# State-space block of a two-layer decoder: the rows of a state are spread two states ahead of their use, and the low-rank rows are copied ahead of the decays

## The reference

```python
xz = layernorm(x) @ W_in;  x_in, z = split(xz)
xc = silu(causal_conv4(x_in) @ pw_kernel + conv_bias)         # 512 inner channels
x_dbl = xc @ W_x                                              # 16 + 8 + 8 columns
delta = softplus(x_dbl[..., :16] @ W_dt + b_dt)
Bm, C = x_dbl[..., 16:24], x_dbl[..., 24:]                    # 8 states
h[t]  = exp(delta[t] * A) * h[t-1] + delta[t] * Bm[t] * xc[t] # per channel and state
y[t]  = sum over the 8 states of C[t] * h[t]
x = x + ((y + xc * D) * silu(z)) @ W_out
```

## Time and profile before

| what | us |
|---|---|
| median of three runs | 3070.16 |
| the profiled execution, own time | 3073.5 |
| its span | 3071.7 |
| state-space groups, first scan to last gating | about 105 to 774 |
| TensorE busy, whole span | 2722.0 (89%) |
| VectorE busy, whole span | 1997.4 (65%) |
| ScalarE busy, whole span | 1518.1 (49%) |
| mean granted TensorE clock | 0.928 |

### The profile page before, as it was taken

One profiled execution on the slowest core, in us unless ns is written; L12 is line 12 of the kernel. 1 busy time (PEld: TensorE's weight loads), 2 busy tenths in 40 slices (PEclk: granted clock), 3 DMA queues, 4 the chain that ended last, 5 costly groups with the idle time before them and its releaser, 6 DMA issues. The chain is left out here.

```text
span 3071.7 us, 60127 instructions
## 1 busy us (share of the span) xinstructions
PE 2722.0 (89%) x20702; PEld 1767.6 (58%) x20703; DVE 1997.4 (65%) x4542; ACT 1518.1 (49%) x2982; POOL 454.4 (15%) x482
## 2 busy tenths in 40 slices
PE   6899999996799999999876689999999799969993
PEld 3344444443466676766665347777777645556662
DVE  2588888888367777777555447777777555653334
ACT  2666666663156666666443136666666233302222
POOL 0000000000300000000033111000110032324441
PEclk9899999997899999999877789999999899969997
DMA  4000000000100000000000100000000120001225
GB/s 112 0 1 0 0 0 0 0 0 0 35 21 20 20 15 20 20 20 15 1 15 1 39 11 26 20 20 20 20 25 11 49 83 20 14 26 61 63 61 165
DMA packets 57938, 80.70 MB, mean 26 GB/s; under 512 B 8880, under 2 KB 47059, under 8 KB 57491
## 3 DMA queue, kind: packets, MB, share of 16 engines
q1 hardware_dynamic: 51778, 62.69, 7.2%
q0 software_dynamic: 6048, 16.52, 1.7%
HBM read 63.59 MB, written 15.60 MB: 26 GB/s over the span
## 5 line engine op out<-in xcount | busy, mean ns | idle before, releaser
L1120 DVE CUSTOM_DVE_ANT_0 xa_h_scores<-xa_h_score_bank,xa_h_added 112x375 f32<-112x375 f32 x1024 | 518.1, 544 | 148.5 <-PE xa_h_score_bank L1055 133.6
L1214 ACT ACTIVATE xa_h_probs<-xa_h_scores,xa_h_negmax 112x375 f32<-112x375 f32 x1024 | 561.4, 600 | 0.9 <-DVE xa_h_negmax L1127 0.6
L1067 PEld LDWEIGHTS xa_h_turn_bank<-keep_ident,xa_h_probs 112*125 112x125 f32 x3072 | 398.6, 190 | 91.4 <-DVE xa_h_probs_t L1134 22.2
L1067 PE MATMUL xa_h_turn_bank<-keep_ident,xa_h_probs 112*125 112x112 f32 x3072 | 438.5, 279 | 8.8 <-DVE xa_h_probs_t L1134 8.5
L1134 DVE COPY xa_h_probs_t<-xa_h_turn_bank 125x448 f32<-125x448 f32 x512 | 319.1, 623 | 150.9 <-PE xa_h_turn_bank L1067 137.6
L1220 ACT ACTIVATE xa_h_probs_t<-xa_h_turn_bank 125x448 f32<-125x448 f32 x256 | 138.6, 541 | 304.5 <-PE xa_h_turn_bank L1067 304.5
L464 PE MATMUL mb_y_bank<-mb_read_out,keep_ident 128*128 128x448 f32 x512 | 231.7, 601 | 30.3 <-DVE mb_read_out L671 30.3
L664 DVE TENSOR_TENSOR_SCAN mb_state<-mb_decay,mb_drive 128x1792 f32<-128x1792 f32 x64 | 253.8, 3965 | 0.2 <-ACT mb_decay L598 0.2
L1055 PE MATMUL xa_h_score_bank<-xa_h_keys,xa_h_queries 32*112 32x375 f32 x2048 | 231.6, 522 | 11.3 <-DVE xa_h_row_max L1120 10.7
L1080 PEld LDWEIGHTS xa_h_sums_bank<-xa_h_probs_t,xa_h_values 125*32 125x32 f32 x6144 | 141.9, 110 | 154.5 <-DVE xa_h_probs_t L1134 149.2
L1080 PE MATMUL xa_h_sums_bank<-xa_h_probs_t,xa_h_values 125*32 125x112 f32 x6144 | 202.7, 265 | 14.6 <-issue 7.3
(11 more groups left out here) (341 smaller groups left out, 4145.7 us busy)
## 6 DMA issues: line engine op xcount, KB each, us to landing
xa_context<-in_ctx_t SPq DMA_DIRECT2D x64, 375.0 KB, 3.1
lm_w<-in_m_w SPq DMA_DIRECT2D x16, 512.0 KB, 9.9
lm_e_wide<-lm_result_rows SPq DMA_DIRECT2D x8, 896.0 KB, 9.8
keep_x<-in_x SPq DMA_DIRECT2D x4, 896.0 KB, 16.0
lm_latent_rows<-lm_rows SPq DMA_DIRECT2D x8, 448.0 KB, 3.2
out_x<-keep_x SPq DMA_DIRECT2D x8, 448.0 KB, 6.3
xa_mask_raw<-in_key_mask SPq DMA_DIRECT2D x1, 1312.5 KB
mb_f_pw<-in_pw SPq DMA_DIRECT2D x1, 1024.0 KB
```

The costliest lines, as they stand in the source:

```text
L1067: last = pe.transpose(turn_bank[(par + kc) % 2][0:KP, g * S:(g + 1) * S], probs[par][:, g, kc * KP:(kc + 1) * KP], keep.ident[0:S, 0:S])
L1120: dve.tensor_tensor_reduce(scores[par][:, g, :], score_bank[g][0:S, 0:SK], added[s][:, :], 1.0, -BIG, ALU.add, ALU.max, row_max[par][:, g: ...
L1214: act.activation(probs[par][:, g, :], scores[par][:, g, :], ACT.Exp, bias=negmax[s][:, G * c + g:G * c + g + 1]).then_inc(probs_ready, 1)
```

## The change

On TensorE each spread moves. The spread of state n + 1 no longer opens turn n; the spread of state n + 2 is issued in turn n instead, after the turn's other matmuls and just before `add_state(g, n)`. So that this starts right, the next group's state 1 is spread at the end of turn 7, behind the second half of the projection, and for group 0 before the groups begin. On ScalarE `read_low` moves from behind `decays(g, n + 2)` to before it, in turn 5. The number of instructions of each kind stays what it was.

```diff
@@ TensorE, group
                 for n in range(N):
-                    if n + 1 < N:
-                        spread(g, n + 1)
                     if n == 0:
                         gate(g)
...
                             spread(g + 1, 0)
                         project_out(g, 1) if not first else pass_over(OUT_B)
+                        if not final:
+                            spread(g + 1, 1)
+                    if n + 2 < N:
+                        spread(g, n + 2)
                     add_state(g, n)
...
             spread(0, 0)
+            spread(0, 1)
             all_groups(pe, group)
@@ ScalarE, group
                         if not final:
                             read_rows(g)
+                    if n == 5 and not final:
+                        read_low(g)
                     if n + 2 < N:
                         decays(g, n + 2)
...
                     if n == 4:
                         read_inner(g, (2, 3))
-                    if n == 5:
-                        read_low(g)
                     if n == 6:
                         cast_first(g)
                         softplus(g)
```

## The result

The changed kernel takes 3046.2 us in the median of four runs (3037.34 to 3051.94), the kernel before 3070.51 us (3066.61 to 3071.97). The ratio is 0.9921, 95% interval 0.9907 to 0.9935: 24.3 us less, where 24.1 were forecast.

A forecast was written before the change was run, and what follows sets the result against it. TensorE was taken to bound the middle groups' states 1 to 4, the read-out-to-product round trip the last group. Savings of 11.2 + 6 x 2.05 + 0.65 = 24.1 us from 3070.2 gave 3046 us, range 3032 to 3060.

The forecast's parts named there:

- Last group: Push leaves the read-out-to-product round trip; scans start 7.65 us apart, 46.6 us from scan 1 to 7; 11.2 us saved.
- States 1 to 4: Middle groups: TensorE bounds at 9.40 us a state in either order, nothing saved; product's row wait near zero in states 3 to 6.
- Group 0: First group, without projection: delta already comes near the logarithm's end, so only softplus starting 0.65 us earlier counts.
- States 5 to 7 of the middle groups: Rows come earlier, low-rank's wait of 0.44 goes, delta starts at the logarithm's end: 2.05 us saved in each of six groups.
- From delta to the gates of the next group the chain is unchanged: Seam between groups: nothing changes there, so each of groups 1 to 6 keeps its 2.05 us, 12.3 in all.
- TensorE loses its clock at the seam: Rival, chance 0.05: longer idling between groups holds half clock through gates to push, 8.1 us a group, giving 3101 us.
- The early low copy: Low-rank result copied ahead of decays, else the spread of state 7 sits behind 1.28 + 2.33 us of exponentials.
- The 331.7: Trace time in us forecast for ScalarE's first copied row of state 7, behind the delayed decays; the product would start there.
- The added wait: TensorE's spread of the next group's state 1 waits 0.9 us for ScalarE's state 0 copy, seven times, hidden.
- The sum: Whole kernel: 11.2 + 6 x 2.05 + 0.65 = 24.1 us saved, so 3046 us.

The follow-up runs named there:

- the two kernels with idle matmuls: Three fp32 matmuls nobody reads before the second half of the gates, groups 0 to 5: on the changed kernel 3039.75 us, on the kernel before 3061.2 us.
- before, last group changed: The kernel before with the spreads ahead of the push in the last group alone, low copy left late: 3056.4 us, ratio 0.9949.
- changed, again: The changed kernel itself, unaltered, measured once more beside the later experiments: 3047.25 us, ratio 0.9928.
- with the spread behind the push: The changed kernel with the spread of the next group's state 1 issued after the push of state 7: 3050.18 us, ratio 0.9923.

## Why the prediction came out

*Last group: right.* Forecast 46.6 us from scan 1 to scan 7, measured 46.5; 11.2 saved, measured 11.9, the tail being 0.6 shorter, as much as the push of state 6 took less (5.71 for 6.34). TensorE's half clock does not matter between the scans, as said.

*States 1 to 4: right.* 9.40 us a state in both, no gain. Only the sign given for it was off: the product's wait for rows did not go near zero there.

*Group 0: right in size.* From first delta to gating 87.67 us before, 87.02 after: 0.65. The run with the low copy late shows that it could have been 1.2 more: the early copy costs that much here.

*States 5 to 7 of the middle groups: the mechanism right, slightly too small.* Forecast 2.05, measured 2.3 (84.98 to 82.64 and 82.71), and 1.8 to 2.25 between the two kernels with idle matmuls. Delta did move to the logarithm's end, 1.66 of the 2.3, and the rows of state 7 were not the last to come. The other 0.6 is low-rank's wait for the row copy: it was priced at its recorded 0.44, but before, low-rank started 0.99 us after the spread in front of it began, where 0.38 is what a spread takes.

*The step that failed is "From delta to the gates of the next group the chain is unchanged".* In waits it is, in clock not. The second half of the gates went from 3.27 to 6.11 in group 1 and from 4.97 to 6.2 or 6.3 in groups 3 and 5, and cost those groups 3.4, 1.7 and 1.7 us (the last two: 1.3 in the gates and 0.4 between low-rank and delta, 21.2 us for 20.84). So the six middle groups gave 7.1 us in the profiled execution where 12.3 were forecast: 5 x 2.3 + 2.5 = 14.0 by the order, less 6.8 by the clock. That the order itself was priced well is shown by the two kernels with idle matmuls, where the gates take 3.2 to 3.3 us on both sides: 11.8 us for groups 1 to 6 against the forecast of 12.3.

The rival "TensorE loses its clock at the seam" named the place, with a price far too high, as the level is back by the end of the gates. Its reason, a longer wait there, isn't borne out. The wait is longer in group 3 alone (3.18 for 2.57); in groups 1, 2 and 4 it is shorter, in group 5 the same, and the five together are 14.4 us in both traces. Wait before the second half of the gates / its length, in us, for three traces of each order:

| trace | group 1 | group 2 | group 3 | group 4 | group 5 | gates above 3.27, sum |
|---|---|---|---|---|---|---|
| before | 3.52 / 3.28 | 2.75 / 4.97 | 2.57 / 4.97 | 2.40 / 4.97 | 3.18 / 4.97 | 6.8 |
| before, low copy early | 3.52 / 4.97 | 3.18 / 3.27 | 2.71 / 4.97 | 2.52 / 4.97 | 2.35 / 4.97 | 6.8 |
| before, last group changed | 3.52 / 4.97 | 3.18 / 3.27 | 2.67 / 4.97 | 2.49 / 4.97 | 3.18 / 4.97 | 6.8 |
| changed | 3.21 / 6.11 | 2.48 / 4.89 | 3.18 / 6.23 | 2.31 / 4.97 | 3.18 / 6.31 | 12.2 |
| changed, again | 3.40 / 3.28 | 3.18 / 4.67 | 3.18 / 6.12 | 2.46 / 4.90 | 3.18 / 6.24 | 8.9 |
| changed, low copy late | 3.06 / 4.91 | 3.18 / 6.24 | 2.29 / 4.97 | 3.18 / 6.32 | 2.25 / 4.97 | 11.1 |

In these traces the gates always lose more in the new order than in the old one (the two traces not shown, with the last group in the old order and with the spread behind the push, have 11.9 and 11.7), so the loss comes with the order. The idle matmuls show that it needs the wait. Why the same wait costs more in the new order stays open.

*The early low copy.* Forecast: without it the spread of state 7 would sit behind 1.28 + 2.33 us of exponentials. That was wrong. The lead that the other edit gives lets ScalarE finish the decays first; with or without the copy ahead the time of the middle groups is the same, and group 0 pays 1.2 us for it. The 331.7 that I worked out for the first row was right. Counted from the start of low-rank it is 7.93 us by the forecast and 7.94 in the trace (324.42 to 332.36), and it is the decays, as forecast, that the row copy stands behind: they end at 331.90, while the spread of 330.88 was done at 331.42. With the low copy late the product starts 0.5 us sooner (7.43), which is hidden, since delta waits for the logarithm in both. The drain that the Trainium skill (ScalarE: Activation LUTs, What ACT_TABLE_LOAD costs) puts beside a table load does not appear in the trace after either: the load of 328.27 starts within 0.02 us of the copy's end, and its exponentials start 1.29 us later, at 329.56.

*The added wait.* Forecast 0.9 us seven times, hidden. Hidden it is, but it is there in group 0 alone. The push of state 6 still runs at a lowered clock (4.97 us) in the middle groups, and delays the projection past the copy.

*The sum: partly luck.* Inside the stage, first delta to last gating, the trace gives 19.7 us; the span 21.6; the medians 24.3. From first to last gating the three traces of stages in this order give 19.0, 22.8 and, with the low copy late, 21.0, so the stage explains about 21 of the 24. The rest of the program was 2 us shorter in one trace of the changed kernel and 8 in the other, and the cause of that was not found. That the medians moved by just what was forecast is therefore not a confirmation of the sum to the microsecond.

## What to carry to other kernels

In this kernel one engine fills a bank, a second copies it out, a third works on it, and the first then adds the result up. Putting the next fill in front of that adding-up takes it out of the round trip. It pays in full where the round trip is the bound (here the last group, 11.9 us in eight states), it pays a part where another engine hands over to the chain (1.8 to 2.5 us a middle group), and it pays nothing where the filling engine itself is busy throughout (states 1 to 4).

Of a second edit made in the same breath, ask what the first does to the order in which things are ready; here it made the second one pointless, and harmful in group 0. And look at the granted clock at every place where an engine waits, also where the wait stays as long as it was: filling that gap with work nobody reads was worth 1.7 us a group in the old order and up to 3.4 in the new one, which is of the size of the reordering itself.

## What the runs showed of the hardware

- The level at which TensorE comes back after a gap is not settled by the gap alone. After one and the same wait of 3.18 us the gates took 3.27 us (group 2 with the low copy early on the kernel before), 4.97 (group 5 before) and 6.23 (group 3 changed), at granted clocks of 1.0, 0.66 and 0.52 over the gates. After 3.52 us they took 3.28 or 4.97, and 2.31 us were enough for 4.97. In the changed order 4.9 and 6.2 mostly alternate from group to group, in the old one 4.97 came three or four times in a row. With the gap cut to under 1 us they took 3.2 to 3.3 in groups 1 to 5 of every kernel with idle matmuls.
- The four timed runs with three idle matmuls lie within 3.1 us (3038.88 to 3042.02), those of the changed kernel within 14.6 and 10.9. That fits draws of the clock at the seams as one cause of the spread, but four runs don't show it, and it can't be the only one: of the 12.2 us between the changed kernel's two traces, 6.0 lie behind the stage.
- VectorE's scan of state 7 takes 3.88 us in groups 1 to 6 of the changed kernel instead of 4.75, while GpSimd's second subtraction of the split takes 1.90 to 2.41 instead of 1.02. The two rows below are those of group 2:

```profile
337.08 3.88 DVE L667 TENSOR_TENSOR_SCAN mb_state<-mb_decay,mb_drive 128x1792 f32<-128x1792 f32 x1
...
339.37 2.41 POOL L382 TENSOR_TENSOR mb_low_parts<-mb_rest,mb_low_parts 32x448 bf16<-32x448 f32 x1 [4.10 <-ACT mb_low_parts L573]
```

The subtraction ends at 341.78, 0.82 us after the scan, as it does within 0.01 in all six groups. In the kernel before it began at 339.44, 0.02 us ahead of the scan, ran its 1.02, and the scan came out 0.87 longer. Each time the one that started second came out longer, and the first took its usual time. This is what the Trainium skill states (SBUF — State Buffer, SBUF: two separate sides) of the port pair that VectorE and GpSimd share: an exclusive lock held for the whole instruction. The trace agrees, for a scan too, and GpSimd's loss here is not on the path: delta waits for the logarithm.
